# Four chained convolution blocks on one core: stores of the first five lattice cells moved to ScalarE's queue, the input stored in three parts, 14 matmuls on zeros ahead of the first cell

## The chip, the cores and the metric

One Trainium2 chip, one core of it. The metric is the device time of the whole program in microseconds, the lower the better: 1303.49 us is the median of three runs before the change (1298.91 to 1303.87).

## What is computed

The reference takes x (8 images, 16 channels, 64 x 64, float32) through four residual blocks, each on a group-normalised x:

```python
x = x + _L0_conv_ref(_gn(x), L0_conv_W, L0_conv_b)
x = x + _L1_conv_ref(_gn(x), L1_conv_weight)
x = x + _L2_conv_ref(_gn(x), ...)      # splines of 3x3 patches
x = x + _L3_conv_ref(_gn(x), ...)
```

The first one is a lattice of 16 cells, and the change lies in its first five:

```python
for col in range(NUM_COLS):          # 4
    for row in range(NUM_ROWS):      # 4
        if col == 0:
            ins = [input_tensor] if row == 0 else [outs[row - 1][-1]]
        elif row == 0:
            ins = [outs[row][0], outs[row + 1][1]]
        elif row == NUM_ROWS - 1:
            ins = [outs[row][0], outs[row - 1][-1]]
        else:
            ins = [outs[row][0], outs[row + 1][1], outs[row - 1][-1]]
        outs[row] = _cell(W[col, row], b[col, row], ins)
```

A cell is a 3 x 3 convolution from up to 48 channels to 48, with bias and ReLU, split into right, up and down.

## The kernel before, in words

All sixteen cells k run one after the other, and each over the eight images b: `s = 8 * k + b` is a step, 128 in all. Every engine runs the same loop over the steps in its own order, and semaphores tie them together. One step goes through five stations:

- SP (SyncE) loads the step's input from an internal array in HBM, `lattice`, into a raw slot of the tile S (`input_loads`, L795). There are four slots (`SLOTS_K`). Cells of kind "12" (one input, two outputs used: cells 0 and 3) take 3 DMAs a step, cells of kind "13" (cells 1 and 2) 6, of kind "22" (cell 4, 7, 8) 6, of kind "33" (cells 5, 6) 16 and two slots. A load waits until the slot was read (`raw_read` or `lo_ready`), and until the cell that makes its input has stored that image (`image_stored`).
- ACT (ScalarE) rounds the raw input into the tile F (`split_hi`, L1136), two pieces ahead of the step that it evacuates. A step has one piece, in kind "33" two.
- DVE (VectorE) makes the remainder, raw minus rounded (`split_lo`, L1437 to L1449), and copies pieces to other partitions.
- PE (TensorE) runs the step's matmuls, 128 x 512 each (`cell_step`, L1711): 12 in kind "12", 20 in "13", 24 in "22", 56 in "33". It writes a ring of four PSUM banks, and each bank is one chunk.
- ACT evacuates each chunk with bias and ReLU into one of three staging slots of S (`evacuate`, L1147). SP stores the staging slot to `lattice` (`output_stores`, `store_outputs`, L778): two DMAs of 272.5 KB in cells 0, 3 and 4, one of 817.5 KB in cells 1 and 2.

Two orders matter here. On SP the stores of step s - 4 (`STORE_LAG`) stand in the queue behind the loads of step s, and wait there for the evacuation. On ACT a step begins with a wait for the store of step s - 3, whose staging slot it writes next, then comes the split of a later piece, with a wait for its load, and then the evacuations:

```python
if s >= SLOTS_S and (s - SLOTS_S) // B < NC - 1:
    z = s - SLOTS_S
    act.wait_ge(image_stored[z % B], 16 * stores_before[z // B + 1])
...
for h in range(cell.pieces):
    ahead = pieces_before[s] + h + 2
    if ahead < TOTP:
        split_hi(piece_step(ahead), ahead - pieces_before[piece_step(ahead)])
    evacuate(s, range(h * part, (h + 1) * part))
```

Ahead of the steps stands the start. SP loads x in four parts, DVE takes the statistics (L1361), PE forms the group means (L1735), POOL (GpSimd) the scale (L859, L861), and ACT and DVE write the normalised input to XN, which lies in raw slots 2 and 3 (L1119, L1371). XN is then stored to `lattice`: images 0 and 1 by SP (L764), images 2 to 7 by POOL (L985). Meanwhile the weights of cell 0 are turned by PE, split by ACT and DVE (`turned_lo_part`, L1312), stored by POOL (L884) and read back spread out by SP (L760).

POOL also clears S: the staging slots at the start (L844), and in cells 1 and 2 the upper halves of the raw slots (L1011, four memsets), which SP waits for before step 32 (`kr_clear`).

## Time and profile before

| | us |
|---|---|
| median of three runs | 1303.49 |
| lowest, highest | 1298.91, 1303.87 |
| the profiled execution, its own time | 1307.1 |
| its span in the trace | 1304.2 |
| PE busy (matmuls) | 1179.5 (90%) |
| DVE busy | 772.4 (59%) |
| ACT busy | 671.2 (51%) |
| POOL busy | 382.3 (29%) |
| moved by DMA | 234.22 MB, mean 180 GB/s |

The span runs from the first to the last instruction of the program in the trace, and the own time is the same execution as the device reports it. Busy shares are means over stages with different limits, so a stage has to be read by itself. SP's work is issuing DMAs, which isn't counted as busy, and shows as SPq.

### The profile page before, as it was taken

To read this page: it belongs to the slowest core of one execution; us is meant where nothing else is said; L and a number is where in the kernel's file an instruction comes from. 1 tells how busy PE (TensorE), PEld (TensorE's weight loads), DVE (VectorE), ACT (ScalarE), POOL (GpSimd) and SP (SyncE) were. 2 spreads that over 40 slices of the span, in tenths; PEclk is the share of its full clock that TensorE was granted. 3 is DMA by queue.
4 is the path that set the end of the run, shared out by engine and by line. 5 is a ranking of instruction groups with operands and counts; after the bars stand their busy time and mean duration, and the time that the engine had idled before them with its cause. 6 is when DMAs were issued, how large, how long until landed. Compare 5 with 4: busy or idle time off the path is not lost.

```text
span 1304.2 us, 14844 instructions
## 1 busy us (share of the span) xinstructions
PE 1179.5 (90%) x5088; PEld 874.7 (67%) x5088; DVE 772.4 (59%) x959; ACT 671.2 (51%) x720; POOL 382.3 (29%) x549
## 2 busy tenths in 40 slices
PE   1778999899999999989999999999999857999995
PEld 1645567666666677766666677877777645777773
DVE  5788972346656522236555552236665579899962
ACT  1567754335454444444454543434445498789821
POOL 5222532335420103321213213634134441103212
PEclk9989999899999999999999999999999878999998
DMA  6689988999999958889999987978799214677783
GB/s 177 167 212 237 270 245 236 197 178 178 217 208 207 221 167 211 223 189 211 196 204 185 194 226 202 252 203 227 192 209 178 47 25 71 94 116 112 117 125 57
DMA packets 106191, 234.22 MB, mean 180 GB/s; under 512 B 38388, under 2 KB 52292, under 8 KB 97668
## 3 DMA queue, kind: packets, MB, share of 16 engines
q1 hardware_dynamic: 89536, 207.02, 70.2%
q0 software_dynamic: 16032, 25.98, 10.5%
q8 instruction: 40, 0.66, 0.2%
q14 instruction: 35, 0.29, 0.1%
q10 hardware_dynamic: 548, 0.27, 0.1%
HBM read 124.15 MB, written 85.75 MB: 161 GB/s over the span
## 4 chain that ended last, share of the span: by engine, by line
PE 54%; SPq 16%; DVE 12%; DMA 6%; issue 5%; ACT 5%; POOL 1%; ACTq 0%; DVEq 0%; POOLq 0%
PE PB L1711 46%; SPq L795 13%; PE PB L1680 6%; DMA S<-lattice 2%; SPq L778 2%; ACT F L1136 2%; DMA lattice<-S 2%; DVE S L1548 2%; DVE S L1542 2%; DVE F L1535 1%; DVE S L1555 1%; DVE F L1437 1%; DMA F<-F 1%; DVE F L1449 1%; SPq L826 1%
## 5 line engine op out<-in xcount | busy, mean ns | idle before, releaser
L1711 PE MATMUL PB<-F,WA 128*96 128x512 f32 (+1 forms) x3792 | 923.8, 405 | 53.0 <-DVE F L1449 32.7
L1711 PEld LDWEIGHTS PB<-F,WA 128*96 128x96 f32 (+1 forms) x3792 | 665.7, 177 | 302.0 <-issue 49.4
L1136 ACT ACTIVATE F<-S 128x2116 fp32r<-128x2116 f32 (+4 forms) x160 | 261.7, 1636 | 240.9 <-issue 87.2
L1147 ACT ACTIVATE S<-PB,BIAS 96x512 f32<-96x512 f32 (+1 forms) x320 | 210.3, 680 | 280.3 <-PE PB L1711 279.9
L1437 DVE TENSOR_TENSOR F<-S,F 128x1089 fp32r<-128x1089 f32 (+2 forms) x80 | 121.4, 1518 | 189.7 <-ACT F L1136 189.3
L1439 DVE TENSOR_TENSOR F<-S,F 128x1058 fp32r<-128x1058 f32 x64 | 80.7, 1262 | 191.2 <-ACT F L1136 190.8
L1449 DVE CAST F<-F 64x528 fp32r<-64x528 f32 (+4 forms) x304 | 186.7, 663 | 3.5
L1680 PE MATMUL PB<-F,WA 128*128 128x512 f32 x576 | 149.5, 419 | 20.3 <-DVE F L1535 20.1
L892 POOL DMA_DIRECT2D WA<-taps x76 | 56.6, 746 | 340.0 <-ACT S L1147 321.7
L1680 PEld LDWEIGHTS PB<-F,WA 128*128 128x128 f32 x576 | 114.2, 200 | 49.9 <-issue 21.5
L1440 DVE TENSOR_TENSOR F<-S,F 64x1058 fp32r<-64x1058 f32 x64 | 82.0, 1281 | 0.0
L884 POOL DMA_DIRECT2D taps<-WX x112 | 67.9, 655 | 18.1 <-ACT S L1147 13.2
L859 POOL TENSOR_TENSOR RS<-VE,NHALF 128x1 f32<-128x1 f32 x25 | 24.4, 975 | 134.7 <-DVE VE L1335 134.6
L877 POOL MEMSET WX<- 48x1600 f32 x18 | 26.3, 1460 | 106.8 <-ACT S L1147 92.3
L1244 ACT ACTIVATE F<-S 128x2112 fp32r<-128x2112 f32 x16 | 31.5, 1967 | 27.8 <-DVE S L1555 14.9
L1443 DVE TENSOR_TENSOR F<-S,F 128x1089 fp32r<-128x1089 f32 x16 | 20.7, 1296 | 40.3 <-ACT F L1136 40.2
L1680 PE MATMUL PB<-F,WX 128*128 128x512 f32 x96 | 31.5, 490 | 13.6 <-DMA F<-F 13.6
L1119 ACT ACTIVATE KAN<-X,NBI,RS 64x512 f32<-64x512 f32 (+1 forms) x48 | 32.5, 676 | 20.2 <-POOL NBI L861 11.2
L1220 ACT ACTIVATE S<-KS,CB 128x528 f32<-128x528 f32 x64 | 41.8, 724 | 0.3
L1535 DVE SCALAR_TENSOR_TENSOR F<-S,F 128x1056 fp32r<-128x1056 f32 x32 | 38.9, 1259 | 3.6 <-ACT F L1244 3.6
L1080 POOL DMA_DIRECT2D out<-OT x26 | 14.7, 571 | 85.5 <-DVE OT L1523 85.5
L1542 DVE SCALAR_TENSOR_TENSOR S<-S 128x2112 f32<-128x2112 f32 x16 | 37.6, 2353 | 2.4 <-ACT S L1228 2.4
(125 smaller groups left out, 717.7 us busy)
## 6 DMA issues: line engine op xcount, KB each, us to landing
lattice<-S SPq DMA_DIRECT2D x48, 817.5 KB, 6.0
S<-lattice SPq DMA_DIRECT2D x448, 66.1 KB, 4.9
lattice<-S SPq DMA_DIRECT2D x98, 272.5 KB, 4.0
S<-lattice SPq DMA_DIRECT2D x160, 136.1 KB, 3.4
S<-lattice SPq DMA_DIRECT2D x72, 272.5 KB, 5.3
S<-lattice SPq DMA_DIRECT2D x160, 70.1 KB, 3.0
S<-lattice SPq DMA_DIRECT2D x80, 136.2 KB, 5.1
S<-lattice SPq DMA_DIRECT2D x160, 66.0 KB, 3.0
```

Source lines behind the costliest of these rows:

```text
L795: sp.dma_start(dst, src).then_inc(image_loaded[q], 16)
L884: pool.dma_start(dst, src).then_inc(tp_stored, 16)
L892: pool.dma_start(dst, src).then_inc(w_loaded[k % 2], 16)
L1136: act.activation(piece_view(s, h, 0), raw_view(s, h), ACT.Copy).then_inc(hi_ready, 1)
L1147: act.activation(wide(to[:, at:at + TS])[:, :, 0:RX], pixels(RING_BANK[n % SLOTS_O][0:cell.rows, :]), ACT.Relu, bias=BIAS[0:cell.rows, k:k ...
L1437: last = nc.vector.tensor_tensor(lo, raw, hi, ALU.subtract)
L1439: nc.vector.tensor_tensor(lo[:, 0:2], raw[:, 0:2], hi[:, 0:2], ALU.subtract)
L1440: last = nc.vector.tensor_tensor(lo[0:4 * C, 2:4], raw[0:4 * C, 2:4], hi[0:4 * C, 2:4], ALU.subtract)
L1449: last = nc.vector.tensor_copy(FP[4 * C:P, slot, part, to:to + n], FP[0:4 * C, slot, 0, source:source + n])
L1542: nc.vector.scalar_tensor_tensor(A2[n % 2], AA[n % 2], 2.0, A2[n % 2], ALU.subtract, ALU.mult)\
L1680: last = nc.tensor.matmul(pixels(bank[:, :]), weights, moving, start=open_ and n == 0, stop=close and n == len(todo) - 1)
L1711: last = nc.tensor.matmul(bank, WA[0:rows, first:first + cell.rows], wide(FZ[0:rows, i % SLOTS_F, base:base + TS])[:, :, 0:RX], start=j == ...
```

## The change

It does five things.

1. ACT stores the outputs of cells 0 to 4 (`ACT_STORED = 5`): in step s, behind the split and ahead of the evacuations, it waits for the evacuation of step s - 1 and issues its stores. SP stores from cell 5 on, as before, four steps late.
2. The normalised input goes to HBM in three parts (`INPUT_PARTS`), all by SP: images 0 and 1, images 2 and 3, and, behind the loads of images 0 and 1, images 4 to 7.
3. The raw slots 0 and 1 are cleared whole by POOL at the start, ahead of the staging slots; the four memsets in cells 1 and 2 and DVE's clear of the gaps go.
4. DVE makes the low part of cell 0's taps behind the first four statistics, and the product with G behind the first six, where both stood ahead of all.
5. PE runs 14 matmuls of 128 x 512 on the tile W3, which DVE now clears whole, into a bank that isn't read, ahead of the first cell.

```diff
-FIRST = 2
+INPUT_PARTS = (0, 2, 4, 8)
+ACT_STORED = 5
...
-        input_stored = [sem(f"input_stored{i}") for i in range(2)]
+        input_stored = [sem(f"input_stored{i}") for i in range(3)]
...
         def input_stores(i):
-            rows = slice(0, FIRST * C) if i == 0 else slice(FIRST * C, P)
+            rows = slice(INPUT_PARTS[i] * C, INPUT_PARTS[i + 1] * C)
...
             sp.wait_ge(xn_act, 1)
             sp.wait_ge(xn_dve, 1)
-            for dst, src in input_stores(0):
-                sp.dma_start(dst, src).then_inc(input_stored[0], 16)
+            for i in range(2):
+                for dst, src in input_stores(i):
+                    sp.dma_start(dst, src).then_inc(input_stored[i], 16)
...
-                if s // B < NC - 1:
+                if ACT_STORED <= s // B < NC - 1:
                     sp.wait_ge(evac_done, chunks_before[s + 1])
                     for dst, src in output_stores(s):
                         sp.dma_start(dst, src).then_inc(image_stored[s % B], 16)
...
+                if s == 0:
+                    sp.wait_ge(kr_clear, 1)
...
-                if s == 4 * B:
-                    sp.wait_ge(kr_clear, 4)
+                if k == 0 and b == 2:
+                    for dst, src in input_stores(2):
+                        sp.dma_start(dst, src).then_inc(input_stored[2], 16)
                 if k == 0:
-                    sp.wait_ge(input_stored[0 if b < FIRST else 1], 2 * 16)
+                    sp.wait_ge(input_stored[b // 2 if b < 4 else 2], 2 * 16)
+                if s == 2:
+                    sp.wait_ge(input_stored[2], 2 * 16)
                 else:
                     sp.wait_ge(image_stored[b], 16 * stores_before[k])
...
+            pool.memset(flat[:, 0:2 * PIECE], 0.0).then_inc(kr_clear, 1)
             pool.memset(ST[:, :, :], 0.0).then_inc(st_clear, 1)
...
-            pool.wait_ge(xn_act, 1)
-            pool.wait_ge(xn_dve, 1)
-            for dst, src in input_stores(1):
-                pool.dma_start(dst, src).then_inc(input_stored[1], 16)
...
-                if k in (1, 2) and b in (1, 3):
-                    half = 2 * (k - 1) + b // 2
-                    pool.memset(flat[4 * C:P, half * PIECE:(half + 1) * PIECE], 0.0).then_inc(kr_clear, 1)
...
+                    if h == 0 and 0 < s <= ACT_STORED * B:
+                        act.wait_ge(evac_done, chunks_before[s])
+                        for dst, src in output_stores(s - 1):
+                            act.dma_start(dst, src).then_inc(image_stored[(s - 1) % B], 16)
                     evacuate(s, range(h * part, (h + 1) * part))
...
-            gaps = flat[:, 0:2 * PIECE].rearrange("p (t f) -> p t f", t=4)
-            nc.vector.memset(gaps[:, :, LEAD:HOFF], 0.0)
...
-                nc.vector.memset(W3[4 * C:P, :, 2:4].bitcast(F32), 0.0).then_inc(wa_clear, 1)
+                nc.vector.memset(W3[:, :, :, :].bitcast(F32), 0.0).then_inc(wa_clear, 1)
...
-            turned_lo_part("cell0")
...
+                if b == 4:
+                    turned_lo_part("cell0")
+                if b == 6:
+                    pair_means()
                 last = nc.vector.bn_stats(STATS[:, b], XC[:, b * PIX:(b + 1) * PIX])
...
+            for i in range(14):
+                nc.tensor.matmul(PB[2][:, :], W3[:, 0, 0], W3[:, 0].rearrange("p t m -> p (t m)"),
+                                 start=True, stop=True)
```

SP's queue at the last images of cell 0 and the first of cell 1, before. A row is one DMA or a run of equal ones; the loads read `lattice` into S, the stores write `lattice`:

```order
L795 DMA S<-lattice 32x1089 [waits input_stored1,raw_read]
L795 DMA S<-lattice 32x561
L795 DMA S<-lattice 32x528
L778 DMA lattice<-S 64x1090 [waits evac_done]
L778 DMA lattice<-S 64x1090
L795 DMA S<-lattice 16x2180 [waits image_stored0,raw_read]
L795 DMA S<-lattice 16x2180
L795 DMA S<-lattice 16x2x529 x4
L778 DMA lattice<-S 64x1090 [waits evac_done]
L778 DMA lattice<-S 64x1090
```

The same place with the change:

```order
L801 DMA S<-lattice 32x1089 [waits image_stored7,input_stored2,raw_read]
L801 DMA S<-lattice 32x561
L801 DMA S<-lattice 32x528
L801 DMA S<-lattice 16x2180 [waits image_stored0,raw_read]
L801 DMA S<-lattice 16x2180
L801 DMA S<-lattice 16x2x529 x4
L801 DMA S<-lattice 16x2180 [waits image_stored1,raw_read]
L801 DMA S<-lattice 16x2180
L801 DMA S<-lattice 16x2x529 x4
```

The stores, and with them the waits for an evacuation, have left the queue; the loads of one step follow those of the step before. ACT's queue at steps 6 to 8 before, where L1136 is a split and L1147 an evacuation:

```order
L1136 ACTIVATE F<-S 64x2180 [waits out_done,image_loaded0,image_stored3]
L1147 ACTIVATE S<-PB,BIAS 128x16x32 [waits out_done] x2
L1136 ACTIVATE F<-S 64x2180 [waits out_done,image_loaded1,image_stored4]
L1147 ACTIVATE S<-PB,BIAS 128x16x32 [waits out_done] x2
L1136 ACTIVATE F<-S 64x2180 [waits out_done,image_loaded2,image_stored5]
L1147 ACTIVATE S<-PB,BIAS 96x16x32 [waits out_done] x4
```

And with the change:

```order
L1136 ACTIVATE F<-S 64x2180 [waits out_done,image_loaded0,image_stored3]
L1194 DMA lattice<-S 64x1090 [waits evac_done]
L1194 DMA lattice<-S 64x1090
L1147 ACTIVATE S<-PB,BIAS 128x16x32 [waits out_done] x2
L1136 ACTIVATE F<-S 64x2180 [waits out_done,image_loaded1,image_stored4]
L1194 DMA lattice<-S 64x1090 [waits evac_done]
L1194 DMA lattice<-S 64x1090
L1147 ACTIVATE S<-PB,BIAS 128x16x32 [waits out_done] x2
```

Between each split and the evacuations behind it stand now the stores of the step before. DVE's order at the start, with the change, where L1302 clears XN, L1368 are the statistics, L1314 is the low part of cell 0's taps and L1357 the product with G (before, these two stood ahead of all eight statistics):

```order
L1302 MEMSET S 128x4360
L1368 BN_STATS STATS<-X 128x6 [waits channel_loaded0]
L1368 BN_STATS STATS<-X 128x6
L1368 BN_STATS STATS<-X 128x6 [waits channel_loaded1]
L1368 BN_STATS STATS<-X 128x6
L1314 TENSOR_TENSOR WX<-PB,WX 16x3x96 [waits turned_hi,channel_loaded2]
L1368 BN_STATS STATS<-X 128x6 x2
L1357 TENSOR_TENSOR KS<-G,CB 128x128 [waits const_loaded,channel_loaded3]
L1368 BN_STATS STATS<-X 128x6 x2
```

## Rows read from the trace of the kernel before

**Rows 1.** The page: busy time of PE, and the chain that ended last by engine

```profile
PE 1179.5 (90%) x5088; PEld 874.7 (67%) x5088; DVE 772.4 (59%) x959; ACT 671.2 (51%) x720; POOL 382.3 (29%) x549
...
PE 54%; SPq 16%; DVE 12%; DMA 6%; issue 5%; ACT 5%; POOL 1%; ACTq 0%; DVEq 0%; POOLq 0%
```

**Rows 2.** Windows by cell (start:end length, busy us, TensorE clock, DMA share, GB/s)

```profile
38.00:72.75 34.75, 26.89 (x114) 20.41 (x115) 25.38 (x26) 17.90 (x22) 8.74 (x13) 0.97 0.67 176
72.75:168.70 95.95, 83.81 (x360) 54.85 (x361) 88.44 (x68) 69.79 (x86) 32.89 (x34) 0.98 0.95 244
140.00:170.00 30.00, 28.21 (x129) 19.03 (x129) 28.22 (x26) 24.49 (x33) 10.50 (x13) 1.00 0.97 272
168.70:203.50 34.80, 29.62 (x125) 22.36 (x124) 20.87 (x21) 18.60 (x25) 10.97 (x13) 0.95 0.86 236
203.50:254.20 50.70, 44.79 (x199) 35.36 (x197) 12.59 (x14) 20.73 (x25) 11.59 (x17) 0.97 0.89 217
254.20:369.50 115.30, 112.85 (x488) 77.25 (x489) 67.20 (x85) 50.72 (x50) 52.77 (x87) 0.97 1.02 191
```

**Rows 3.** The chain that ended last, in order of time (start us, us, what)

```profile
10.20 4.76 DVE STATS L1361 x8
...
28.14 5.97 DMA S<-lattice
...
38.10 5.35 PE PB L1711 x12
...
342.03 66.65 PE PB L1711 x280
```

**Rows 4.** Timeline in cell 1, steps 12 and 13 (start us, us, what)

```profile
99.55 5.19 SPq L795 DMA_DIRECT2D S<-lattice  x6
...
100.76 2.56 DVE L1449 CAST F<-F 64x2180 fp32r<-64x2180 f32 x3
```

**Rows 5.** SP queue's waits, 72.7 to 168.7 us (us in total, times, longest)

```profile
SPq L778 <- ACT S L1147: 6.0, 12, 1.3
```

**Rows 6.** Issues of L795, 72.7 to 168.7 us (ns min/median/max of one issue)

```profile
L795 SPq DMA_DIRECT2D S<-lattice x85: 370/592/2938, 72.7 to 168.2; - x85
...
DMA to landing us min/median/max: 2.9/4.6/6.5
```

**Rows 7.** Groups of lines, 72.7 to 168.7 us (busy, mean ns, idle before)

```profile
L1711 PE MATMUL PB<-F,WA 128*96 128x512 f32 x320 | 81.2, 410 | 18.8 <-ACT S L1147 10.2 <-DVE F L1449 8.3
...
L1437 DVE TENSOR_TENSOR F<-S,F 64x2180 fp32r<-64x2180 f32 x15 | 36.3, 2419 | 6.7 <-ACT F L1136 6.5
L1136 ACT ACTIVATE F<-S 64x2180 fp32r<-64x2180 f32 x15 | 30.4, 2024 | 26.8 <-issue 26.8
```

**Rows 8.** PE's timeline: first matmuls of cells 0, 1 and 5

```profile
38.10 11.07 PE L1711 MATMUL PB<-F,WA 128*128 128x512 f32 x36 [14.75 <-DVE F L1449]
...
72.75 7.45 PE L1711 MATMUL PB<-F,WA 128*96 128x512 f32 x21 [6.68 <-DVE F L1449]
...
254.15 42.00 PE L1711 MATMUL PB<-F,WA 128*96 128x512 f32 x168 [5.91 <-DVE F L1449]
```

**Rows 9.** ACT's timeline at the end of cell 4

```profile
248.04 1.97 ACT L1136 ACTIVATE F<-S 128x2116 fp32r<-128x2116 f32 x1 [10.54 <-DMA S<-lattice]
249.92 1.25 ACT L1147 ACTIVATE S<-PB,BIAS 128x512 f32<-128x512 f32 x2
```

**Rows 10.** Timeline of the start: DVE and SP

```profile
3.52 3.69 DVE L1300 MEMSET S<- 128x4360 f32 x1 [0.86 <-issue]
...
15.47 5.19 SPq L760 DMA_DIRECT2D WA<-taps  x8
...
25.78 12.04 SPq L795 DMA_DIRECT2D S<-lattice  x15
44.19 1.15 SPq L778 DMA_DIRECT2D lattice<-S  x2
```

**Rows 11.** DMA issues, 170 to 200 us (count, KB each, median us to landing)

```profile
lattice<-S SPq DMA_DIRECT2D x12, 272.5 KB, 3.7
```

More of the change, by code:

```diff
@@ L1352, in tail, with pair_means @@
                 group_stats(slice(n % B, n % B + 1), n)
-            dve.wait_ge(const_loaded, 2 * 16)
-            nc.vector.tensor_tensor(PAIR_MEAN.rearrange("p (b c) -> p b c", c=C),
-                                    G[:, :].rearrange("p (b c) -> p b c", c=C),
-                                    OWN.rearrange("p (b c) -> p b c", c=1).broadcast_to([P, B, C]), ALU.mult)
+            def pair_means():
+                dve.wait_ge(const_loaded, 2 * 16)
+                nc.vector.tensor_tensor(PAIR_MEAN.rearrange("p (b c) -> p b c", c=C),
+                                        G[:, :].rearrange("p (b c) -> p b c", c=C),
+                                        OWN.rearrange("p (b c) -> p b c", c=1).broadcast_to([P, B, C]), ALU.mult)
             for b in range(B):
```

## The prediction

> **What bounds the kernel now.** Start with the page. TensorE (PE) is busy 90% of the span, yet the chain that ended last gives it only 54%; 16% of that chain is SPq, SyncE's queue issuing transfers [rows 1]. An average hides stages, so the windows view by cell comes next [rows 2]. In cell 5 PE is busy 112.9 of 115.3 us. In the stretches before, it is busy 26.9 of 34.8 (cell 0), 83.8 of 96.0 (cells 1 and 2), 29.6 of 34.8 (cell 3) and 44.8 of 50.7 (cell 4). What the change can win lies almost wholly in front of 254 us. A matmul of the lattice costs 66.65 / 280 = 0.238 us in the middle of cell 5 to 6, and 5.35 / 12 = 0.446 us in the first image of cell 0 [rows 3].
>
> Then SP's queue. In a step of cell 1 its six loads take 5.19 us; the step's store and the next six loads follow without a pause [rows 4]. In the whole of cells 1 and 2 SP waits 6.0 us before its stores, out of 96 [rows 5]. So it hardly waits: it issues. One load's issue takes 0.59 us in the median and up to 2.94 [rows 6]. Now who waits for whom there: PE stood idle 18.8 us, for ACT and DVE, and ACT 26.8 us before its splits, the instructions that stand behind a load [rows 7]. DVE, 88.4 of 96.0 us, is the fullest engine beside SP [rows 2].
>
> The clearest single stall is in front of cell 5's first matmul at 254.15: PE idles 5.9 us [rows 8], because ACT had waited 10.5 us for the sixteen loads of cell 5's first image [rows 9], and two evacuations of cell 4 stood behind that split. The loads were late because the queue was.
>
> **The change part by part.** The profiled execution took 1307.1 us, the median of the three runs is 1303.49, 0.3% less. I sum against the span, 1304.2, and take the difference off the median.
>
> *Start: -4.3 us.* DVE's statistics wait now for G and begin at 10.2, though its clear ends at 3.52 + 3.69 = 7.2 [rows 3, 10]. They will begin at 7.2 and carry two small instructions (the low part of cell 0's taps and the product with G, I take 0.8 us for both): 4.8 + 0.8 ends at 12.8 instead of 14.96. POOL's clear of 4360 more columns ends near 10 and stands ahead of nothing before that. But the low part of the taps now stands behind four statistics and comes 0.8 us later, so SP's 5.19 us of cell 0's weights run from about 16.2 to 21.4 instead of 15.47 to 20.66 [rows 10]. The input stores queue behind that: at 21.4, where they are at 21.05 now. The 2.2 us are lost again. What remains comes from the traffic. Before, POOL's two stores of 817.5 KB ran beside SP's and ahead of the first loads, and the first images' loads, begun at 25.78, kept ACT waiting until 34.11 [rows 3, 10]: 8.3 us, where a load lands 4.6 us after its issue in cells 1 and 2 [rows 6]. With four stores of 272.5 KB in flight I take loads from 25.2 to 29.8, so PE starts at 33.8 instead of 38.1. Ends: 0 (as slow as now) and -6. The third part goes out behind image 1's loads and lands near 32.5; image 2's loads wait for it, about where they are now.
>
> *The 14 matmuls on zeros: 0.* 14 x 0.446 = 6.2 us, from about 22.4 (where the longer clear of W3 ends) to 28.6. PE stood idle 14.75 us before 38.1 [rows 8], which covers them; were the first cell ready at once they would cost up to 6.2. Could they give the first image the full rate? That is 12 x 0.208 = 2.5 us. After the 6.68 us of idle before cell 1, 21 matmuls took 7.45 us, 0.355 each [rows 8], so part of them ran at the slow rate. My idle is 5.2 us, nearer to that than to none. I take 0, ends 0 and -2.5.
>
> *Rest of cell 0: -8.6.* SP's first store, of image 0, stood at the head of the queue until 44.19 with image 5's loads behind it [rows 10]. With the stores on ACT, SP has three loads a step. Images 2 to 7 follow from 40.4 at 12 x 0.238 = 2.9 us, to 57.8; cell 1's first split is then the next to be late (2.02 us on ACT, 2.42 + 2.56 on DVE [rows 4, 7]), and gives 59.8. From 33.8 that is 26.0; from 38.1 to 72.75 it was 34.65 [rows 8]. Ends -3 and -11.
>
> *Cells 1 and 2: -9.5.* SP loses one store a step and would need 6 x 0.59 = 3.5 us. Next to be late: DVE, 2.42 + 2.56 = 5.0 us a step; PE, 20 x 0.238 = 4.8; the transfer engines: 244 GB/s over 95.95 us are 1.46 MB a step, and at 272 GB/s, the best 30 us that I found [rows 2], that is 5.4 us. I take 16 x 5.4 = 86.4. Ends: 5.05 by DVE (-15), 0 by the transfer engines. On ACT the store's issue, some 0.6 us as on SP, stands behind a split of 2.02 us and can be issued while that runs; the evacuations stand behind it. Without that cover it costs 0.6 a step on an engine busy 69.8 of 96 us, still nothing on the path. POOL's four memsets go; nobody waits for them, 0.
>
> *Cell 3: -7.8.* 8 x 2.86 = 22.9, some 1.8 for a turn of taps, and 2.3 for the stores: two per image, 1.2 us of issue, which a split of one half-size piece only just covers, and ACT's staging slot needs their landing (3.7 us [rows 11]) within two steps of 2.9. 27.0 against 34.8. Ends -3 and -10. *Cell 4: -3.2.* 192 x 0.238 + 1.8 = 47.5 against 50.7. Cell 5's sixteen loads can start when the low part of image 5 is made, some 28 us before PE needs them, and take about 16 x 0.63 + 4.6 = 15. Ends 0 and -3.7. *Cell 5: -5.3.* 448 x 0.238 + 2 = 108.6; I leave 1.4 for its own first store, which still stands behind image 4's loads on SP. 110 against 115.3. Ends 0 and -6.7. From cell 6 on nothing changes.
>
> Sum: 4.3 + 8.6 + 9.5 + 7.8 + 3.2 + 5.3 = 38.7 us. Span 1265.5; from the median, 1303.5 - 38.7 = 1264.8, say **1265 us**.
>
> **Rivals.** *The transfer engines are the bound already.* Their share is 0.95 in cells 1 and 2 [rows 2]. Then cells 1 and 2 give nothing and cell 3 half: 38.7 - 9.5 - 3.9 = 25.3, 1278 us. For: SP's issues of 2.9 us look like a queue held by full engines [rows 6]. Against: at the same share both 244 and 272 GB/s were moved [rows 2]. The Trainium skill, "DMA: Bandwidth & Descriptors", section "Issuing engines are not separate DMA queues", states the rule behind this rival: all issuers end on the same 16 engines, and a second issuer saves only the time that the first needs to initiate. By that rule alone cells 1 and 2 would not move.
>
> *DVE's floor is reached and the first image runs at the full rate:* 5.5 + 2.5 us more, 1257.
>
> *ACT's queue is held: slower.* An evacuation stands behind each store's issue. If ACT's issues take as long as SP's longest, 2.9 us [rows 6], a step with two stores costs 2 x 2.9 + 1.25 (two evacuations [rows 9]) = 7.05 us, against 4.3 in cells 0 and 3 and 6.3 in cell 4: +44 and +6, less the 14.8 of cells 1, 2 and 5: +35, 1338 us. It turns from gain to loss at about 2 us per store. For: both queues feed the same full engines. Against: 0.59 us is the median even at a share of 0.95 [rows 2, 6]. The Trainium skill, "Perfetto Trace Analysis", section "DMA Instruction — HWDGE (DVE, Sync)", says that one queue at a time locks the block that makes descriptors, and that the wait for it counts in the profiled duration; no row of this trace shows both queues at work on full engines. By it ACT's issue would grow by what is left of SP's.
>
> *The change does not move what binds:* SP's loads wait for free slots and landings instead, the front ends as late as now, 1300 us. Against: in cells 1 and 2 a slot is free again 4.4 us after a split begins (2.02 + 2.42 [rows 7]) and is read four steps, 20 us, after that beginning; a group of loads needs 3.5 of issue and 4.6 to land, which leaves 7.
>
> **How the numbers follow.** Forecast 0.55 (own range 1254 to 1274), transfer engines 0.25, deeper floor 0.12, ACT held 0.05, nothing moved 0.03. A measurement of this kernel tells a difference of about 0.5% (6.5 us) from none. Faster 0.92, within it 0.03, slower 0.05. The range 1250 to 1284 takes in the first three with most of their ends.
>
> **What would show it.** Right: the first lattice matmul near 34, cell 1's near 60, cell 2's last evacuation near 147, cell 5's first matmul near 222 with under 2 us of idle before it; SP waiting between its groups of loads; ACT's store issues near 0.6 us and inside the splits; DVE over 90% busy in cells 1 and 2. The first rival: SP's load issues still long, the share at 0.95 and steps of 5.8 us or more. ACT held: store issues of 2 us and PE waiting for evacuations. The forecast as a whole is wrong if cell 5's first matmul comes after 245.

## The result, and the profile after

The changed kernel takes 1283.82 us in the median of four runs, the kernel before 1303.68 in the four beside them: a ratio of 0.9865 (95% interval 0.9839 to 0.9892), 1.35% faster. The forecast was 1265 us, 3% faster. The direction came true, at about half the size.

The profiled execution has a span of 1282.3 us, 21.9 less than before. Its page, PE's busy time and the chain that ended last by engine (compare [rows 1]):

```profile
PE 1182.2 (92%) x5102; PEld 877.9 (68%) x5102; DVE 766.0 (60%) x958; ACT 673.5 (53%) x720; POOL 374.6 (29%) x544
...
PE 58%; SPq 15%; DVE 11%; DMA 6%; issue 5%; ACT 3%; POOL 1%; DVEq 0%; ACTq 0%; POOLq 0%
```

SP's queue has lost the 64 transfers that ACT now issues, but only one point of the chain. The windows by stage (columns as in [rows 2]; the borders are the first matmul of cell 0 and of cell 1, the last evacuations of cells 2 and 3, the first matmul of cell 5 and its last evacuation):

```profile
0.00:37.00 37.00, 9.48 (x56) 7.63 (x57) 22.40 (x59) 7.28 (x9) 20.30 (x27) 0.95 0.65 158
37.00:69.50 32.50, 27.33 (x115) 20.93 (x115) 25.23 (x27) 20.79 (x25) 8.42 (x13) 0.90 0.85 241
69.50:158.10 88.60, 84.37 (x360) 56.98 (x361) 82.75 (x68) 69.12 (x83) 24.81 (x30) 0.94 0.99 262
158.10:190.00 31.90, 30.09 (x135) 23.32 (x133) 20.70 (x21) 19.28 (x25) 10.58 (x13) 1.00 0.93 259
190.00:234.40 44.40, 42.30 (x186) 33.32 (x187) 12.46 (x14) 21.10 (x26) 11.60 (x17) 1.00 0.92 247
234.40:348.60 114.20, 112.67 (x488) 77.02 (x489) 69.20 (x87) 50.92 (x51) 51.53 (x87) 0.97 1.03 187
```

Against the stages before, with what was foretold:

| stage | before | foretold | after | gain foretold | gain |
|---|---|---|---|---|---|
| to the first lattice matmul | 38.1 | 33.8 | 37.0 | 4.3 | 1.1 |
| cell 0, to cell 1's first matmul | 34.65 | 26.0 | 32.5 | 8.6 | 2.2 |
| cells 1 and 2 | 95.95 | 86.4 | 88.6 | 9.5 | 7.4 |
| cells 3 and 4 | 85.5 | 74.5 | 76.3 | 11.0 | 9.2 |
| cell 5 | 115.3 | 110.0 | 114.2 | 5.3 | 1.1 |
| the rest | 934.7 | 934.7 | 933.7 | 0 | 1.0 |

Two places hold most of the miss: the first 70 us (9.6 us short) and cell 5 (4.2 us short). The start first, SP's timeline (start us, us, what; compare [rows 10]):

```profile
16.27 5.33 SPq L761 DMA_DIRECT2D WA<-taps  x8
21.72 3.98 SPq L766 DMA_DIRECT2D lattice<-S  x4
27.08 4.67 SPq L801 DMA_DIRECT2D S<-lattice  x6
31.80 1.15 SPq L793 DMA_DIRECT2D lattice<-S  x2
38.90 4.03 SPq L801 DMA_DIRECT2D S<-lattice  x9
```

The weights and the input stores go out where they were expected (16.2 and 21.4). From there each landing is late. The first loads go out at 27.08 and not at 25.2, because the first part of the input needs 5.3 us to land (21.72 to 27.03). ACT's first split is at 33.06, 6.0 us behind the first load's issue. The third part, issued at 31.80, holds SP until 38.90: 7.1 us. Image 2's loads write the raw slot in which this part still lies, so they wait for its landing at 38.84. SP's waits, 16 to 69 us (us in total, times, longest), name it; L797 is the wait for the third part:

```profile
SPq L761 <- DMA taps<-WX: 8.4, 1, 8.4
SPq L797 <- DMA lattice<-S: 5.9, 1, 5.9
SPq L799 <- DMA lattice<-S: 3.6, 2, 2.3
```

ACT's timeline shows what that does to the splits (L1136): 7.0 us of idle in front of image 2's.

```profile
33.06 2.11 ACT L1136 ACTIVATE F<-S 64x1089 fp32r<-64x1089 f32 x2 [13.68 <-DMA S<-lattice]
42.17 1.12 ACT L1136 ACTIVATE F<-S 64x1089 fp32r<-64x1089 f32 x1 [7.00 <-DMA S<-lattice]
```

PE's timeline at the same place and in front of cells 1 and 5 (compare [rows 8]):

```profile
23.05 5.04 PE L1753 MATMUL PB<-W 128*128 128x512 f32 x14 [1.59 <-DVE W L1309]
37.02 7.34 PE L1718 MATMUL PB<-F,WA 128*128 128x512 f32 x24 [8.94 <-DVE F L1456]
46.21 4.60 PE L1718 MATMUL PB<-F,WA 128*128 128x512 f32 x12 [1.85 <-ACT F L1136]
...
69.48 5.77 PE L1718 MATMUL PB<-F,WA 128*96 128x512 f32 x17 [3.30 <-DVE F L1456]
...
234.40 2.17 PE L1718 MATMUL PB<-F,WA 128*96 128x512 f32 x5 [1.97 <-DVE F L1456]
```

The stall before cell 5 is down from 5.91 us to 1.97. In cells 1 and 2 SP still hardly waits between its loads, 2.3 us in 88.6, and its issues have not become shorter: 0.63 us in the median against 0.59, 1.01 in the mean against 0.92. SP issues for 83.7 of the 88.6 us. Its waits there, and the single issues of the loads (L801) and of ACT's stores (L1194) with their landings (ns min/median/max; compare [rows 5, 6]):

```profile
SPq L801 <- DVE F L1444: 2.3, 4, 0.8
```

```profile
L801 SPq DMA_DIRECT2D S<-lattice x83: 376/630/2762, 69.4 to 157.7; - x83
...
DMA to landing us min/median/max: 2.8/5.1/9.1
```

```profile
L1194 ACTq DMA_DIRECT2D lattice<-S x18: 310/311/619, 71.3 to 158.1; - x18
...
DMA to landing us min/median/max: 3.7/6.2/7.8
```

### The profile page after: what moved, and what is told of

It reads as the page before. It is cut to its first block, busy times and chain, and to the rows that moved or that the text cites. A ratio compares the mean times of both kernels' runs of the same rounds, so it can differ in the third digit from the quotient of the medians.

```text
span 1282.3 us, 14874 instructions
## 1 busy us (share of the span) xinstructions
PE 1182.2 (92%) x5102; PEld 877.9 (68%) x5102; DVE 766.0 (60%) x958; ACT 673.5 (53%) x720; POOL 374.6 (29%) x544
## 3 DMA queue, kind: packets, MB, share of 16 engines
q1 hardware_dynamic: 84160, 181.90, 65.7%
## 4 chain that ended last, share of the span: by engine, by line
PE 58%; SPq 15%; DVE 11%; DMA 6%; issue 5%; ACT 3%; POOL 1%; DVEq 0%; ACTq 0%; POOLq 0%
PE PB L1718 50%; SPq L801 12%; PE PB L1687 6%; DMA S<-lattice 3%; DVE S L1555 2%; DVE S L1549 2%; DVE F L1542 1%; DVE S L1562 1%; ACT F L1136 1%; DMA lattice<-S 1%; DMA F<-F 1%; SPq L780 1%; SPq L832 1%; PE PB L1678 1%; ACT KAN L1119 1%
## 5 line engine op out<-in xcount | busy, mean ns | idle before, releaser
L1147 ACT ACTIVATE S<-PB,BIAS 96x512 f32<-96x512 f32 (+1 forms) x320 | 213.3, 683 | 302.5 <-PE PB L1718 299.6
L1136 ACT ACTIVATE F<-S 128x2116 fp32r<-128x2116 f32 (+4 forms) x160 | 261.4, 1634 | 196.4 <-DMA S<-lattice 81.4
L1446 DVE TENSOR_TENSOR F<-S,F 128x1058 fp32r<-128x1058 f32 x64 | 80.7, 1261 | 187.6 <-ACT F L1136 187.1
L1456 DVE CAST F<-F 64x528 fp32r<-64x528 f32 (+4 forms) x304 | 181.4, 646 | 3.5
L884 POOL MEMSET WX<- 48x1600 f32 x18 | 25.9, 1437 | 108.4 <-ACT S L1147 94.9
L1119 ACT ACTIVATE KAN<-X,NBI,RS 64x512 f32<-64x512 f32 (+1 forms) x48 | 32.5, 676 | 20.2 <-POOL NBI L868 11.2
## 6 DMA issues: line engine op xcount, KB each, us to landing
S<-lattice SPq DMA_DIRECT2D x72, 272.5 KB, 5.1
lattice<-S SPq DMA_DIRECT2D x52, 272.5 KB, 4.1
lattice<-S ACTq DMA_DIRECT2D x48, 272.5 KB, 5.1
```

The lines of the kernel that those rows point to most:

```text
L1136: act.activation(piece_view(s, h, 0), raw_view(s, h), ACT.Copy).then_inc(hi_ready, 1)
L1147: act.activation(wide(to[:, at:at + TS])[:, :, 0:RX], pixels(RING_BANK[n % SLOTS_O][0:cell.rows, :]), ACT.Relu, bias=BIAS[0:cell.rows, k:k ...
L1446: nc.vector.tensor_tensor(lo[:, 0:2], raw[:, 0:2], hi[:, 0:2], ALU.subtract)
L1456: last = nc.vector.tensor_copy(FP[4 * C:P, slot, part, to:to + n], FP[0:4 * C, slot, 0, source:source + n])
```

## The experiments

Each is built on the changed kernel, save where the kernel before is named. Ratios are to the kernel before, measured beside it; the changed kernel stands at 0.9865 [0.9839, 0.9892]. Stage times are of one trace each.

**The moved stores alone.** The kernel before, with the third item of this diff alone:

```diff
+ACT_STORED = 5
...
-                if s // B < NC - 1:
+                if ACT_STORED <= s // B < NC - 1:
...
+                    if h == 0 and 0 < s <= ACT_STORED * B:
+                        act.wait_ge(evac_done, chunks_before[s])
+                        for dst, src in output_stores(s - 1):
+                            act.dma_start(dst, src).then_inc(image_stored[(s - 1) % B], 16)
```

> The kernel before with the moved stores alone (ACT stores cells 0 to 4); input in two parts, POOL's memsets and DVE's order as before, no matmuls on zeros. Theory A (the moved stores bring the gain, and the input in three parts holds cell 0 back, since image 2's loads wait until 38.8 us for the third part): first lattice matmul near 38, cell 1's first matmul near 66 (69.5 in the changed kernel), and 1279 to 1284 us in all, as fast as the changed kernel or faster. Rival B (the three parts, the early statistics and the memsets that are gone bring a good part of the 20 us): cell 1's first matmul after 70, 1290 us or more.

Measured: 1282.57 us, ratio 0.9848 [0.9824, 0.9872]. The whole gain is there. The first matmul comes at 38.8 and cell 1's at 67.2, as theory A has it: a later start than in the changed kernel (37.0) and an earlier end of cell 0 (69.5).

**The rest of the change without them.**

```diff
-ACT_STORED = 5
+ACT_STORED = 0
```

> The changed kernel with the stores of cells 0 to 4 back on SP, four steps late; all other parts of the change kept. Theory A: the other parts bring nothing or cost a few us, 1300 to 1308 us. Rival B: they bring 6 us or more, 1297 us or less.

Measured: 1300.51 us, ratio 0.9992 [0.9977, 1.0007]. With the stores on SP, input in three parts, earlier statistics, cleared slots and the zeros together are worth nothing that shows.

**The input in two parts, the second by POOL as before.**

```diff
-INPUT_PARTS = (0, 2, 4, 8)
+INPUT_PARTS = (0, 2, 8)
...
+            pool.wait_ge(xn_act, 1)
+            pool.wait_ge(xn_dve, 1)
+            for dst, src in input_stores(1):
+                pool.dma_start(dst, src).then_inc(input_stored[1], 16)
```

> The changed kernel with the input stored in two parts as before (images 0 and 1 by SP, images 2 to 7 by POOL); all else as in the changed kernel. Theory A: image 2's loads begin near 31 instead of 38.9 us, cell 1's first matmul comes at 64 to 66 instead of 69.5, and the time is 3 to 5 us below the changed kernel's, 1279 to 1281. Rival C (the larger store in front of the first loads delays image 0 by as much as image 2 gains, or what is gained ahead of cell 1 is waited for later on full transfer engines): first lattice matmul at 38 or later, within 2 us of the changed kernel in all.

Measured: 1284.76 us, 0.9881 [0.9859, 0.9902]. SP's own input stores now take 5.13 us to issue for two, behind POOL's, and the first matmul comes at 40.7. The end is where it was, as rival C has it.

**Without the matmuls on zeros.**

```diff
-            for i in range(14):
-                nc.tensor.matmul(PB[2][:, :], W3[:, 0, 0], W3[:, 0].rearrange("p t m -> p (t m)"),
-                                 start=True, stop=True)
```

> The changed kernel without the 14 matmuls on zeros. The granted clock of the changed kernel rose to full at 26.5 us, fell at 33.3 and rose again at 40.1, 3.1 us after the first lattice matmul. Theory: without them the first image's matmuls run at the slow rate for some 5 us as before, but PE waits for image 2 after two images anyway, so cell 1's first matmul moves by less than 0.5 us and the time by less than 1. Rival: they keep a slow stretch away that is on the path, 2 us or more slower without them.

Measured: 1282.9 us, 0.9849 [0.9827, 0.9870]. The zeros gain nothing that can be measured. PE's first 24 matmuls take 7.48 us, with the zeros 7.34:

```profile
36.77 7.48 PE L1718 MATMUL PB<-F,WA 128*128 128x512 f32 x24 [15.31 <-DVE F L1456]
```

**POOL's small loads in cell 6.** One of seven such lines:

```diff
-                if k == 5 and b == 0:
+                if k == 6 and b == 0:
```

> The changed kernel with POOL's 24 small loads of the last layers' weights (and what follows on them) moved from cell 5's eight images to cell 6's. Theory A (cell 5 is late because these transfers fill the engines on top of SP's sixteen loads per image; engine share 1.03 in cell 5): cell 5's loads land in 5 to 6 us instead of 8.1 in the median, ACT's waits for SP's loads in front of its splits shrink from 15 us to under 5, and cell 5 takes 110 to 112 us instead of 114.2. If cell 6 then shows the same stalls, the whole stays within 1282 to 1285; if not, about 1280. Theory B (cell 5's stalls come from its own loads and the order of SP's queue): cell 5 still takes 113.5 us or more, with ACT waiting 12 us or more.

Measured: 1283.26 us, 0.9859 [0.9834, 0.9884]. In the trace cell 5 takes 111.1 us in place of 114.2 (the last stage's window); the median doesn't follow. On the kernel before with the stores moved, the same edit:

> The kernel before with two edits alone: the stores of cells 0 to 4 by ScalarE (as in the run of the moved stores alone), and POOL's small loads of the last layers' weights in cell 6 instead of cell 5. Theory A (these loads cost cell 5 some 3 us, as the one trace of that run had it, 111.1 against 114.2, and cell 6 has room, 107.9 in both): cell 5 takes 110 to 111.5 us, ratio to before about 0.0025 under that of the moved stores alone, 1279 to 1281. Theory B (that difference was the spread of single traces, since the median moved by 0.5 us): 1282 to 1284, cell 5 at 112 to 113.

Measured: 1284.94 us, 0.9872 [0.9849, 0.9894], with 110.5 us for cell 5 in the trace. Both profiled executions were the shortest of their kernels (1281.63 and 1279.73), which may flatter their stages; but their cell 5 is as long as theory A has it, and only the medians speak for theory B. With the run of all three small edits below, cell 5 takes 109.5 to 111.1 us in the three traces with this edit, and 110.9 to 118.5 in the eleven without it that read all bytes there. So a gain in cell 5 is likely, none is measured in the whole, and where it goes stays open.

**Cell 5's stores on ACT too.**

```diff
-ACT_STORED = 5
+ACT_STORED = 6
```

> The changed kernel with cell 5's stores moved to ScalarE as well (ACT_STORED = 6). Theory A (a store of SP stands behind the next image's loads and lands 10 us late; the split that reads it waits, 2 to 4 us of PE in cell 5): cell 5 takes 111 to 113 us instead of 114.2, and ACT's wait for the stores there, 25 us, falls under 15: 1280 to 1282. Theory B (the transfer engines are full in cell 5, whoever issues): stores land as late as before, the steps are as long, 1283 to 1285. Rival: an evacuation stands behind ACT's issues, and with the engines full these take 2 us each instead of 0.5: cell 5 grows by 5 us or more, 1288.

Measured: 1289.43 us, 0.9895 [0.9855, 0.9934]; cell 5 took 115.2 us. No gain. The median is the one that the rival named, but its mechanism isn't seen: ACT's issues took 0.33 us in the median there and 0.72 at most. The interval overlaps with the changed kernel's, so a loss isn't shown. ACT's wait has only changed its name, to SP's loads. Its waits in cell 5, after and here:

```profile
ACT F L1136 <- DMA lattice<-S: 25.2, 5, 6.7
ACT F L1136 <- DMA S<-lattice: 15.1, 2, 9.4
```

```profile
ACT F L1136 <- DMA S<-lattice: 35.2, 5, 10.2
```

**Fewer bytes in cells 1 and 2.**

```diff
+            n = 16 if k in (1, 2) else LEAD
-            yield top[:, :, 0:LEAD], odd[:, :, TS:TS + LEAD]
+            yield top[:, :, 0:n], odd[:, :, TS:TS + n]
```

> The changed kernel with the halo loads of cells 1 and 2 cut to 16 columns each; as many issues on every queue, about a fifth fewer bytes per step. It leaves out most of the halo input of cells 1 and 2. Theory A (the 16 transfer engines bind cells 1 and 2: share 0.99 at 262 GB/s, 5.5 us a step): the 88.6 us of cells 1 and 2 fall to 81 to 84, where DVE (5.05 us a step) is next, share under 0.9, and SP begins to wait before its issues: 1276 to 1279. Theory B (SP's issues bind, six loads a step at 0.6 to 0.9 us each, bytes or not): 88 us stay, SP still never waits. Theory C (DVE binds already at 82.75 of 88.6 us): 87 us or more, and SP waits.

Measured: 1281.93 us, 0.9836 [0.9801, 0.9870]. The window of cells 1 and 2:

```profile
66.80:152.50 85.70, 80.68 (x360) 53.89 (x361) 81.41 (x68) 69.86 (x86) 24.34 (x30) 1.00 0.84 235
```

With the share down from 0.99 to 0.84 the two cells take 2.9 us less, where theory A wanted 4.6 to 7.6. No theory fits whole: DVE is busy 81.4 of 85.7 us, and SP waits 1.5 us, so its queue is as full as before. Nor are the 2.9 us shown to be the transfers': PE's matmuls alone took 3.7 us less (84.37 and 80.68) at a granted clock of 1.00 in place of 0.94, and this trace is of the shortest execution of its kernel (1275.82).

**The order at the start.** Three runs. First SP's input stores ahead of cell 0's weights:

```diff
-            for dst, src in cell_spread(cells[0]):
-                sp.dma_start(dst, src).then_inc(w0_loaded, 16)
             sp.wait_ge(xn_act, 1)
             sp.wait_ge(xn_dve, 1)
             for i in range(2):
                 for dst, src in input_stores(i):
                     sp.dma_start(dst, src).then_inc(input_stored[i], 16)
+            for dst, src in cell_spread(cells[0]):
+                sp.dma_start(dst, src).then_inc(w0_loaded, 16)
```

> The changed kernel with SP issuing the first two parts of the input stores ahead of cell 0's weights instead of behind them. Theory A (the first image's chain, store at 21.7, landing 27.0, loads to 33.0, is what sets PE's start; weights are needed only at 37): stores at 19.0, first lattice matmul at 34.5 to 35.5 instead of 37.0, and since cell 0 is then held by the third part and its landing, under 1 us of that reaches the end: 1282 to 1284. Theory B (landings under load set it, not the place in the queue): first matmul still 36 or later, weights become the late ones, no change or 1 us worse.

Measured: 1285.26 us, 0.9874 [0.9825, 0.9923]; first matmul at 37.7. Second, the third part behind the first two:

```diff
-                if k == 0 and b == 2:
+                if k == 0 and b == 0:
                     for dst, src in input_stores(2):
```

> The changed kernel with the third part of the input issued by SP right behind the first two (at about 25.8, where SP only waits for the first part) instead of behind image 1's loads. Theory A (cell 0 is held by the third part, issued at 31.8 and landed at 38.8, with SP idle 5.9 us behind it): it lands near 33.5, the first loads share the engines with it and come 1 to 2 us later, PE starts at 38 to 39, and cell 1's first matmul comes at 66 to 67.5 instead of 69.5: 1281 to 1282. Theory B (the first part of cell 0 is set by the sum of bytes, 2.2 MB of input and the loads behind it, in whatever order): cell 1's first matmul at 69 or later, no change in the time.

Measured: 1286.32 us, 0.9883 [0.9857, 0.9909]; first matmul at 41.5, cell 1's at 70.6. Third, all parts by ACT:

```diff
+            act.wait_ge(xn_act, 1)
+            act.wait_ge(xn_dve, 1)
+            for i in range(3):
+                for dst, src in input_stores(i):
+                    act.dma_start(dst, src).then_inc(input_stored[i], 16)
```

> The changed kernel with all three parts of the input issued by ScalarE right behind its share of the normalisation, at about 19, beside SP's issue of cell 0's weights, instead of by SP behind these. Theory A (SP's place in the queue costs the start 2.7 us, and the third part the rest): the first part lands at 23 to 24, the last near 31, SP's first loads go out at 24, the first lattice matmul at 34.5 to 36 and cell 1's first at 63 to 65 instead of 69.5: 1278 to 1280. Theory B (three parts in flight hold SP's queue, as POOL's two stores did before the change: single issues of 2 us and loads landing 7 us late): first matmul 37 to 38, cell 1's first 66 to 67, 1281.

Measured: 1284.89 us, 0.9861 [0.9829, 0.9893]; first matmul at 37.1, cell 1's at 65.7 in a trace whose execution was the shortest of its kernel. SP's queue in the first of the three, in the second and in the third:

```profile
19.09 2.86 SPq L763 DMA_DIRECT2D lattice<-S  x4
22.00 8.17 SPq L766 DMA_DIRECT2D WA<-taps  x8
30.27 2.84 SPq L801 DMA_DIRECT2D S<-lattice  x6
```

```profile
25.86 4.08 SPq L793 DMA_DIRECT2D lattice<-S  x2
30.04 11.19 SPq L801 DMA_DIRECT2D S<-lattice  x15
```

```profile
16.28 7.19 SPq L761 DMA_DIRECT2D WA<-taps  x8
23.60 13.20 SPq L793 DMA_DIRECT2D S<-lattice  x15
```

Whatever is put behind the input stores is held. Eight loads of weights take 8.17 us there and 5.33 ahead of them; fifteen loads of images take 11.19 or 13.20 us, as they took 12.04 before [rows 10]. In the medians theory B of each came true, no gain. In the traces an order moves the stall: the third run has cell 1's first matmul 3.8 us earlier than the changed kernel, the second 1.1 us later. That the start is set by its bytes fits all three and isn't shown by them, since none has fewer bytes in its stores. No trace has the first matmul before 36.4.

**Half of the load bytes, the same issues.** This and the next tell bytes from issues.

```diff
-        def input_loads(s):
+        def all_loads(s):
...
+        def input_loads(s):
+            for dst, src in all_loads(s):
+                if s < 6 * B:
+                    n = src.shape[-1] // 2
+                    dst, src = (v[..., 0:n] if len(v.shape) == 2 else v[:, :, 0:n] for v in (dst, src))
+                yield dst, src
```

> The changed kernel with every load of cells 0 to 5 cut to the first half of its columns: as many issues on each queue, about a third fewer bytes. It leaves out half of what the lattice reads in cells 0 to 5. Theory A (full transfer engines are all that stood between the forecast and the result: they hold SP's queue and make each load land late): the terms of the prediction that are reckoned on TensorE and VectorE alone come out: cells 1 and 2 in 82 to 84 us (88.6 now), cells 3 and 4 in 74 to 75.5 (76.3), cell 5 in 109 to 111 (114.2), and cell 0, which still waits for the third part of the input, in 28 to 31 (32.5): 1266 to 1272. Theory B (VectorE and the order of waits bind as much as the transfers): cells 1 and 2 in 85.5 us or more, cell 5 in 113 or more, 1278 to 1282, as in the run with short halos.

Measured: 1271.16 us, 0.9780 [0.9763, 0.9797].

```profile
36.50:66.60 30.10, 26.33 (x115) 20.18 (x115) 24.85 (x26) 19.11 (x23) 9.43 (x13) 0.93 0.72 198
66.60:154.30 87.70, 83.48 (x360) 55.85 (x361) 82.27 (x68) 70.19 (x86) 24.70 (x30) 0.96 0.79 223
154.30:183.50 29.20, 28.98 (x132) 22.85 (x131) 20.73 (x21) 19.24 (x26) 10.57 (x13) 1.00 0.88 232
183.50:227.50 44.00, 44.00 (x195) 34.81 (x195) 15.95 (x17) 21.34 (x26) 11.59 (x17) 1.00 0.75 200
227.50:335.90 108.40, 108.40 (x485) 74.70 (x484) 63.45 (x83) 52.51 (x51) 57.05 (x87) 1.00 0.63 152
```

Theory A holds from cell 3 on: PE is busy without a gap in cells 4 and 5, cells 3 and 4 take 73.2 us and cell 5 108.4. It doesn't hold for cells 1 and 2: 87.7 us, with the engines' share at 0.79. There SP's queue is still full. The issues of its loads (L809 in this run) take 0.63 us in the median and 0.93 in the mean, and it waits 2.9 us in all:

```profile
L809 SPq DMA_DIRECT2D S<-lattice x87: 302/632/2412, 66.4 to 153.9; - x87
```

```profile
SPq L809 <- DVE F L1452: 2.9, 4, 1.4
```

ACT sat idle 15.0 us before its splits in these two cells, and each of these waits ended within 0.1 us behind the landing of a load. DVE is busy 82.3 of the 87.7 us. Both are near the limit, and no run parts them.

**The same with the stores on SP.**

```diff
-ACT_STORED = 5
+ACT_STORED = 0
```

> The same with the stores left on SP (ACT_STORED = 0). It leaves out half of what the lattice reads in cells 0 to 5. Theory A (a place behind a store in SP's queue costs only because full engines make each issue and landing long): within 4 us of the run before it, 1268 to 1275. Theory B (SP's queue is a bound by itself: seven issues a step and a store that waits for the last evacuation at its head): 8 us or more behind it, SP waiting for evacuations 6 us and more in cells 1 and 2, and loads issued late though the engines are free.

Measured: 1288.79 us, 0.9918 [0.9903, 0.9933], 17.6 us behind the run before it (15.2 by the spans of the two traces). Theory B holds, but for one sign: in cells 1 and 2 SP waits 3.7 us for evacuations, not 6 or more. Stage by stage, what it costs to leave the stores on SP (us, from the traces' spans of each stage):

| | cell 0 | cells 1, 2 | cell 3 | cell 4 | cell 5 |
|---|---|---|---|---|---|
| with all bytes | 2.9 | 5.5 | 3.2 | 7.6 | -0.7 |
| with half of the load bytes | 3.4 | 3.5 | 3.2 | 5.0 | 3.6 |

So SP's queue is a bound of its own. What part of this is the stores' issues, what part the waits for evacuations at the head of the queue, and what part the place four steps late, these runs don't say: no run has the stores on SP in another order. SP's timeline at the end of cell 4, with the share at 0.65 in that cell, then ACT's:

```profile
217.51 2.85 SPq L809 DMA_DIRECT2D S<-lattice  x5
220.40 1.09 SPq L788 DMA_DIRECT2D lattice<-S  x2
221.59 13.10 SPq L809 DMA_DIRECT2D S<-lattice  x16
234.73 1.23 SPq L788 DMA_DIRECT2D lattice<-S  x2
```

```profile
236.31 1.98 ACT L1144 ACTIVATE F<-S 128x2116 fp32r<-128x2116 f32 x1 [8.41 <-DMA S<-lattice]
```

The sixteen loads begin at 221.59, behind an image's two stores, and take 13.10 us to issue with half the bytes, where before they took 12.64 with all of them. The loads of that cell land 2.3 us after their issue in the median. ACT waits 8.4 us for them, and PE then 3.8. With ACT storing, the same loads are part of one unbroken run of 41 issues that began at 199.43:

```profile
199.43 33.30 SPq L809 DMA_DIRECT2D S<-lattice  x41
```

**All three small edits together.** ACT issuing the input, POOL's small loads in cell 6, no zeros:

> A candidate with what single traces showed as better, on top of the changed kernel: the three input parts issued by ScalarE, the small loads of the last layers in cell 6, no matmuls on zeros. If the transfer engines are the bound up to cell 5 and none of the three takes bytes away, it is not measurably better: 1280 to 1285, ratio 0.983 to 0.987. If the 4 us at the front and 3 us in cell 5 hold in the median: 1275 to 1278, ratio 0.980 to 0.982.

Measured: 1281.7 us, 0.9861 [0.9840, 0.9882]. Its trace is 6.2 us shorter than that of the changed kernel, but it was again the shortest execution of its kernel, and the ratio is the changed kernel's. No version that computes everything beats the changed kernel by what can be measured.

## Why the prediction was wrong in size

**Right: what is won and by which edit.** The prediction gave the moved stores, beside a part of cell 0, the terms of cells 1 to 4, 20.5 us, and 16.6 came; the runs with the stores alone and without them show that the whole gain is theirs. The zeros were put at 0 and are worth 0, ends 0 and -2.5 (14 took 5.04 us, 0.36 each and not 0.446). POOL's and DVE's clears, tried only together with the rest, bring nothing that shows. The rival that ACT's queue is held fell. In cells 1 and 2 its issues took 0.31 us in the median and lay inside the splits. In cells 0, 3 and 4 they took 0.54 to 0.62, and an image's second store often outlasted its split, by 2.8 us at one place in cell 3.

**Wrong: the start, "loads from 25.2 to 29.8".** This step took the landing time of cells 1 and 2's loads, 4.6 us, for the first loads, and 3.8 us (21.4 to 25.2) for the first part of the input. They measured 6.0 and 5.3. The four stores of 272.5 KB in flight, which the step itself named, with the weights before them held the loads, if less than POOL's two had done (8.3 us [rows 3, 10]). First matmul at 37.0, not 33.8. Its pessimistic end, 0, was nearer than its value.

**Wrong: "the third part lands near 32.5".** It landed at 38.84, image 2's loads could go out only at 38.90, and its split came at 42.17. That is the main part of cell 0's miss (-2.2 in place of -8.6). Cell 0 takes 28.4 to 29.4 us in the six traces where nothing of the input goes out behind image 1's loads, and 29.9 to 33.7 in the six with the late third part and all of cell 0's bytes (stores on ACT in all twelve); but what is gained there is lost at the start or in a later stage, for the medians are the same. With the load bytes halved and the third part still late it takes 30.1.

**Nearly right, and partly by luck: cells 1 and 2, 16 x 5.4.** 88.6 us came, 5.5 a step. The reason given, transfer engines at 272 GB/s, is at most the smaller half of it: they moved 262, but with their share down to 0.79 or 0.84 the two cells still took 87.7 and 85.7 us. The step that failed is "SP ... would need 6 x 0.59 = 3.5 us". It priced a queue by the median of its issues; the mean was 0.92 before and 1.01 after, and 0.93 with half the bytes, so six loads take 5.5 to 6.1 us and SP never paused between its groups, which was to be a sign of being right. SP's queue and DVE (5.0 us a step by itself) lie equally near to what came, and the runs don't tell which of them binds.

**Wrong: cell 5, "about 16 x 0.63 + 4.6 = 15".** Sixteen loads issued in 12.64 us before, 0.79 each and not 0.63, and land in 5.9 us in the median within cell 5, up to 12.8, at an engines' share of 1.03. The store that was to cost 1.4 lands 10.3 us after its issue at 275.60. SP waits 20.8 us for slots in that cell, so its queue has room. The landings are late and the slots few; with half the bytes loads land in 2.6 us and cell 5 takes 108.4, a little better than the 110 foretold. Of the 5.8 us between 114.2 and 108.4 PE's idle time inside the cell is only 1.5. The other 4.3 are the same 488 matmuls, busy 112.67 and 108.40 us, at a granted clock of 0.97 and 1.00: behind the waits of 1.97 and 1.53 us stand stretches at 0.70 and 0.73. The first of them (the last three numbers are clock, DMA share, GB/s):

```profile
234.40:240.00 5.60, 5.60 (x18) 3.73 (x19) 3.60 (x5) 0.03 (x1) 4.83 (x9) 0.70 1.15 211
```

The prediction reckoned such waits as idle time alone. Cells 3 and 4 fell 1.8 us short of their term, and with half the bytes beat it by 1.3.

**The sum.** 38.7 us were reckoned, 21.9 came in the span. With half the load bytes it was 1304.2 - 1271.8 = 32.4. So 10.5 of the missing 16.8 us are the load bytes on full transfer engines (11 by the ratios). Of the other 6.3, the front makes up all and cells 3 to 5 give some back: with half the load bytes the first matmul still came at 36.5 in place of 33.8, and cell 0 took 30.1 in place of 26.0. That this is the input's own bytes is argued from the runs on its order and not shown; it would need the input's stores cut as well.

**The rivals.** The first, transfer engines the bound already (1278), was the nearest in time and named the cause, but in the wrong place: it gave cells 1 and 2 nothing, where 7.4 us came, and left the start and cell 5 whole, where they bound. The Trainium skill, "DMA: Bandwidth & Descriptors", section "Issuing engines are not separate DMA queues", says that a second issuer saves only the sequencer's time for initiating. The trace agrees with the rule and not with the price that I hung on it: a store's place in SP's queue is worth 17.6 us here with the engines partly free (15.2 by the spans), and 16.9, by the spans, with them full (1299.2 without the moved stores, 1282.3 with them). Where one queue's list of transfers has no pause in it, the time of initiating is on the path. As to the lock that one issuer holds (the Trainium skill, "Perfetto Trace Analysis", section "DMA Instruction — HWDGE (DVE, Sync)"), ACT's issues in cells 1 and 2 don't show it: 0.62 us at most beside SP's of up to 2.76. In cell 3 one took 2.20 us, so the runs don't rule it out.

## What to carry to other kernels

A queue that issues without a pause can be a bound even where its transfers could go faster: moving one kind of transfer to an engine with idle time gained 1.35%, although the transfer engines were at a share of 0.95. Price such a queue by the mean of its issues and not by the median (0.92 and 0.59 us here). Once the engines' share is near 1, price a load by what it takes to land among the bytes in flight at that very place, not by the median of another stage; and expect a changed order of the same bytes to move the stall, not to remove it. Before you believe a stage of one trace, see where its execution stands among the runs: here the single runs of one kernel lay up to 13 us apart, more than any of the small edits could bring.

## What was not expected of the hardware

- Issuing a load costs SP the same with half its bytes: 592 ns in the median of cell 5 in both, and 13.10 us for sixteen in the run with half bytes and stores on SP, against 12.64 before.
- Two queues that issue side by side can hold each other up: with ACT's six input stores issued from 19.09 (5.84 us), SP's eight weight loads took 7.19 us in place of 5.33.
- The granted clock of cells 1 and 2 was 0.94 in the changed kernel and 1.00 with short halos, and the same 360 matmuls took 84.4 and 80.7 us. PE's waits, the one in front of cell 1's first matmul included, came to about the same, 7.5 and 7.1 us. In the changed kernel they were three of 1.8 to 3.3 us, each followed by a stretch at a granted clock of 0.63 to 0.74; with short halos they were eight of 0.3 to 2.2 us, and the clock stayed at 1.00.
